# Graph network on one core: tiles moved from the counted part of stage 1 to that of stage 2, with passes, node pieces and first indices placed anew

## What is computed

```python
# layer 0: two SAGE convolutions (mean over the in-edges), then residual and layernorm
h = relu(x @ Ws1 + mean_agg(x, src, dst) @ Wn1 + b1)
h = h @ Ws2 + mean_agg(h, src, dst) @ Wn2 + b2
x = layernorm(x + h)
# layer 1: an edge network, messages summed by dst, then residual and layernorm
ef  = (relu(edge_attr @ We1 + be1) @ We2 + be2) * sigmoid(edge_weight @ Wt + bt)
msg = relu(concat([x[src], ef]) @ Wm1 + bm1) @ Wm2 + bm2
out = layernorm(segment_sum(msg, dst) + x + x)      # all in float32
```

## Time and profile before

| | |
|---|---|
| median of 3 runs | 7867.11 us (7864.79 to 7884.57) |
| profiled execution | 7882.65 us, span 7881.0 us |
| busy in the span | PE 76%, DVE 62%, ACT 48%, POOL 73% |
| first gathers of the stages | 3.58, 2279.25 and 3908.13 us |
| last gathers of stages 1 and 2 | 2206.78 and 3857.70 us |

### The profile page before, as it was taken

How to read it: one execution, slowest core, us unless ns; L and a number is a source line. 1 busy time by engine, 2 the same in 40 slices (tenths; PEclk the granted TensorE clock), 3 DMA queues, 4 the chain that set the end, 5 groups by cost and what they waited for, 6 DMA issues and landing times. The chain is left out here.

```text
span 7881.0 us, 109150 instructions
## 1 busy us (share of the span) xinstructions
PE 5987.7 (76%) x32520; PEld 3927.2 (50%) x32520; DVE 4860.4 (62%) x9745; ACT 3780.1 (48%) x6514; POOL 5733.1 (73%) x5857
## 2 busy tenths in 40 slices
PE   5778888888768788887677777777777777777777
PEld 4555555555545555565444444444444444444444
DVE  8999888888745555555365455555555555555555
ACT  2111121222120000000177777777888888888887
POOL 7777776666547777777577777777777777777776
PEclk8888998999879989898788888888888888888888
DMA  4466777887768898898644444444444444444443
GB/s 123 145 208 227 241 258 257 288 286 269 258 206 301 299 307 299 299 313 301 207 131 133 129 134 130 135 133 132 133 134 134 134 133 136 133 138 137 135 134 105
DMA packets 651285, 1524.09 MB, mean 193 GB/s; under 512 B 162961, under 2 KB 346917, under 8 KB 643014
## 3 DMA queue, kind: packets, MB, share of 16 engines
q1 hardware_dynamic: 463491, 1133.19, 42.7%
q0 software_dynamic: 187200, 383.76, 17.2%
HBM read 1374.92 MB, written 141.47 MB: 192 GB/s over the span
## 5 line engine op out<-in xcount | busy, mean ns | idle before, releaser
L1709 POOL DMA_INDIRECT messages_rows<-y_d,src_idx x3125 | 2991.6, 957 | 1001.5 <-issue 944.4
L1112 POOL DMA_INDIRECT sum_x_rows<-in_x,sum_x_edges x1525 | 1577.4, 1034 | 628.1 <-issue 434.4
L1112 POOL DMA_INDIRECT sum_z_rows<-z_d,sum_z_edges x1200 | 1162.7, 969 | 488.2 <-issue 345.4
L1787 PE MATMUL messages_p_msg<-Wm_e,messages_gated 128*128 128x128 f32 x6250 | 1009.9, 328 | 511.0 <-DVE messages_below L1926 510.5
L1787 PEld LDWEIGHTS messages_p_msg<-Wm_e,messages_gated 128*128 128x128 f32 x6250 | 934.3, 237 | 889.3 <-issue 888.0
L1916 DVE TENSOR_TENSOR messages_p_msg<-messages_p_msg,messages_rows 128x1024 f32<-128x1024 f32 x391 | 481.3, 1231 | 1172.0 <-DMA messages_rows<-y_d,src_idx 930.3
L1216 PE MATMUL sum_x_build<-sum_x_key_hot,sum_x_low_hot 128*128 128x490 bf16 (+2 forms) x2900 | 831.2, 373 | 300.3 <-DVE sum_x_counts L1412 289.9
L1307 ACT CAST sum_x_hot<-sum_x_hot 128x320 bf16<-128x320 f32 x305 | 139.7, 458 | 1739.8 <-DVE sum_x_hot L976 1739.8
L1812 ACT ACTIVATE messages_hot<-iota,rel 128x128 bf16<-128x128 f32 x3125 | 950.2, 389 | 0.0
L1236 PE MATMUL sum_z_p_loaded<-sum_z_split,sum_z_counts 128*128 128x384 bf16 x2744 | 799.3, 350 | 161.5 <-DMA sum_z_split<-z_parts_d 156.2
L1799 PE MATMUL messages_p_edge<-messages_hid,We 128*128 128x512 f32 x1564 | 804.2, 640 | 0.0
(11 more groups left out here) (274 smaller groups left out, 9251.5 us busy)
## 6 DMA issues: line engine op xcount, KB each, us to landing
sum_x_split<-x_parts_d SPq DMA_DIRECT2D x392, 675.5 KB
sum_z_split<-z_parts_d SPq DMA_DIRECT2D x392, 675.5 KB
messages_when<-in_edge_weight SPq DMA_DIRECT2D x391, 512.0 KB, 4.1
messages_attr<-in_span_attr SPq DMA_DIRECT2D x391, 256.0 KB
counts_d<-sum_x_counts SPq DMA_DIRECT2D x392, 224.0 KB
sum_z_counts<-counts_d SPq DMA_DIRECT2D x56, 1568.0 KB
messages_rows<-y_d,src_idx POOLq DMA_INDIRECT x3125
sum_x_rows<-in_x,sum_x_edges POOLq DMA_INDIRECT x1525
```

The source lines that it names most:

```text
L1112: nc.gpsimd.indirect_dma_start(out=rows[:, s % depth, j, :], out_offset=None, in_=table, in_offset=bass.IndirectOffsetOnAxis(ap=edges[:, b ...
L1709: nc.gpsimd.indirect_dma_start(out=rows[:, g % SPAN_DEPTH, j, :], out_offset=None, in_=d["y"], in_offset=bass.IndirectOffsetOnAxis(ap=src_ ...
L1787: last = nc.tensor.matmul(p_msg[:, j * P:(j + 1) * P], gated[:, g % SPAN_GATEDS, j * P:(j + 1) * P], t.Wm_e[:], start=True, stop=True)
```

## The change

Five edits, all in the tables and in which tile a gather reads its indices from.

1. Stage 1 counts tiles 0 to 1500 (25 blocks, 13 pieces from counted blocks, units up to slot 308) and gathers 1625. Stage 2 loads 25 blocks and counts 1500 to 1925 itself, in 17 blocks; it still gathers 1200.
2. In stage 2, 18 intervals between ends of its own blocks hold the 25 passes, so 7 of them are cut in two halves with a pass in each, spread evenly; before, all 14 intervals were cut in two, for 28 passes.
3. In stage 1 pieces that start after slot 278 (`units_by - LATE`) follow each other by 4 slots for 5, and pieces of gathered nodes may start 2 slots after their last group for 4.
4. The indices of the first 25 gathers of stage 2 are loaded in stage 1 (`second_src`), and those of the first 24 gathers of stage 3 in stage 2 (`third_src`).
5. The load of `xT` of a stage 1 piece goes from step 0 to step 1.

```diff
-SPAN_LOADS, SPAN_AHEAD = 4, 3
+SPACING_LATE, LATE = 4, 30
+SPAN_LOADS, SPAN_AHEAD, SPAN_FIRST = 4, 3, 3
...
+        extra = plan.loaded - len(ends)
...
-            until = from_ + 16 if last else ends[j + 1]
-            halves = [(from_, until)] if len(left) <= blocks - j + 1 else [(from_, (from_ + until) // 2), ((from_ + until) // 2, until)]
+            double = ((j + 1) * extra + len(ends) // 2) // len(ends) > (j * extra + len(ends) // 2) // len(ends)
+            until = from_ + (16 if double else 8) if last else ends[j + 1]
+            halves = [(from_, (from_ + until) // 2), ((from_ + until) // 2, until)] if double else [(from_, until)]
...
+    def gathered_by(k):
+        tile = tiles * sqrt(min((PIECE * (k + 1) + 80) / m.N, 1.1))
+        return min(int((tile - end) / TILES) + 2, plan.groups)
...
-            tile = tiles * sqrt(min((PIECE * (k + 1) + 80) / m.N, 1.1))
-            ready.append(min(int((tile - end) / TILES) + 4, plan.groups + 2))
+            ready.append(gathered_by(k))
...
-        slot += spacing
+        slot += spacing if slot < units_by - LATE else SPACING_LATE
...
-        if s == 0:
+        if s == 1:
             load(sp, n, k)
...
-                if q == 0:
+                if q == 0 and (first or body):
                     pool.wait_ge(edges_in[body % EDGES_RING], 16 * (body // EDGES_RING + 1))
...
+                if s == UNROLL and first:
+                    sp.dma_start(t.second_src[:], d["edges"][:, second_from // BODY, 0]).then_inc(next_in, 16)
+                if s == UNROLL and not first:
+                    sp.dma_start(t.third_src[:], d["src_tiles"][:, 0:SPAN_FIRST * SPAN]).then_inc(next_in, 16)
...
-    first = make_plan(m, 0, 1600, 28, 14, 290, SPACING)
-    second = make_plan(m, 1600, 1925, 13, 20, 212, SPACING_SECOND, first)
+    first = make_plan(m, 0, 1500, 25, 13, 308, SPACING)
+    second = make_plan(m, 1500, 1925, 17, 20, 212, SPACING_SECOND, first)
```

More of the change, by code:

```diff
@@ L150, in make_plan @@
             from_ = plan.block_end[b]
-            plan.passes.append(([b], from_, min(26, plan.block_end[b + 1] - from_ - 2) if b + 1 < plan.blocks else 9))
+            plan.passes.append(([b], from_, min(26, plan.block_end[b + 1] - from_ - 2) if b + 1 < plan.blocks else 6))
     for together, from_, length in plan.passes:
@@ L161, in nodes_until @@
         return m.N * (tile / tiles) ** 2
+    def gathered_by(k):
+        tile = tiles * sqrt(min((PIECE * (k + 1) + 80) / m.N, 1.1))
+        return min(int((tile - end) / TILES) + 2, plan.groups)
     ready, plan.first_block, plan.last_block = [], [], []
     for k in range(m.PIECES):
-        if k < flat:
-            from_ = next((b for b in range(plan.blocks) if nodes_until(plan.block_at[b]) + P >= PIECE * k - 10), plan.blocks - 1)
+        from_ = next((b for b in range(plan.blocks) if nodes_until(plan.block_at[b]) + P >= PIECE * k - 10), plan.blocks)
+        last = next((b for b in range(plan.blocks) if nodes_until(plan.block_at[b + 1]) >= PIECE * (k + 1) + 10), plan.blocks - 1)
+        if k < flat and from_ < plan.blocks:
             plan.first_block.append(from_)
-            last = next((b for b in range(plan.blocks) if nodes_until(plan.block_at[b + 1]) >= PIECE * (k + 1) + 10), plan.blocks - 1)
             plan.last_block.append(last)
@@ L179, in make_plan @@
         plan.start[k] = slot
-        slot += spacing
-    plan.slots = plan.start[plan.order[-1]] + PIECE_STEPS
+        slot += spacing if slot < units_by - LATE else SPACING_LATE
+    plan.slots = max(plan.start[plan.order[-1]] + PIECE_STEPS, plan.groups + 2)
     assert [k for k in plan.order if k >= flat] == list(range(flat, m.PIECES))
@@ L287, in vector_checks @@
         then(nc.vector.tensor_tensor(above[:, 0:plan.blocks], block_f[:], above[:, 0:plan.blocks], ALU.is_lt))
-        then(nc.vector.tensor_scalar(above[:, plan.blocks:], block_f[:], float(plan.flat * PIECE - P), None, ALU.is_gt))
+        then(nc.vector.tensor_scalar(above[:, plan.blocks:], block_f[:], float(plan.touched * PIECE - P), None, ALU.is_gt))
         then(nc.vector.tensor_reduce(found[:, 4:5], above[:], axis=AX.X, op=ALU.max))
-        then(nc.vector.memset(above[:, 0:plan.blocks], float(plan.flat * PIECE)))
-        for k in reversed(range(plan.flat)):
+        then(nc.vector.memset(above[:, 0:plan.blocks], float(plan.touched * PIECE - P)))
+        for k in reversed(range(plan.touched)):
             if plan.first_block[k]:
@@ L978, in one_hot, with sum_neighbours @@
         rel.unsqueeze(2).to_broadcast([P, TILES, WIN]), ALU.is_equal)
-def sum_neighbours(nc, m, plan, d, t, table, parts, first, nodes_step, sb, pb, sem):
+def sum_neighbours(nc, m, plan, d, t, table, parts, first, nodes_step, second_from, sb, pb, sem):
     C = PARTS if first else 1
@@ L1106, in _ @@
                 wait_for(pool, sums_ready, s - depth + 1)
-                if q == 0:
+                if q == 0 and (first or body):
                     pool.wait_ge(edges_in[body % EDGES_RING], 16 * (body // EDGES_RING + 1))
                 pool.sem_inc(gathers_started, 1)
+                sources = edges[:, body % EDGES_RING, 0] if first or body else t.second_src[:]
                 for j in range(TILES):
@@ L1181, in _ @@
             placed.sync_last(sp)
+            sp.wait_ge(next_in, 16)
             if first:
@@ L1708, in _ @@
                     at = g * SPAN + j
+                    sources = t.third_src[:] if g < SPAN_FIRST else src_idx
                     nc.gpsimd.indirect_dma_start(
                         out=rows[:, g % SPAN_DEPTH, j, :], out_offset=None, in_=d["y"],
-                        in_offset=bass.IndirectOffsetOnAxis(ap=src_idx[:, at:at + 1], axis=0)).then_inc(rows_arrived[g % SPAN_DEPTH], 16)
+                        in_offset=bass.IndirectOffsetOnAxis(ap=sources[:, at:at + 1], axis=0)).then_inc(rows_arrived[g % SPAN_DEPTH], 16)
             for q in range(SPAN_DEPTH):
@@ L2163, in gnn @@
         t.zeros = sb("zeros", [P, 1], FP32)
+        t.second_src, t.third_src = sb("second_src", [P, BODY], I32), sb("third_src", [P, SPAN_FIRST * SPAN], I32)
         t.columns, t.iota = sb("columns", [P, 1024], FP16), sb("iota", [P, P], FP32)
-        run("sum_x_", sum_neighbours, nc, m, first, d, t, d["x"], d["x_parts"], True, first_nodes)
+        run("sum_x_", sum_neighbours, nc, m, first, d, t, d["x"], d["x_parts"], True, first_nodes, second.end)
         where_needed("any_x_", sum_neighbours_generally, nc, m, d, t, d["x"], True, first_nodes)
-        run("sum_z_", sum_neighbours, nc, m, second, d, t, d["z"], d["z_parts"], False, second_nodes)
+        run("sum_z_", sum_neighbours, nc, m, second, d, t, d["z"], d["z_parts"], False, second_nodes, None)
         where_needed("any_z_", sum_neighbours_generally, nc, m, d, t, d["z"], False, second_nodes)
```

11 lines of the change are left out of this document (8 added, 3 removed).

## The result

The changed kernel takes 7837.61 us (median of 20 runs, 7828.46 to 7857.74), the kernel before 7867.86 us (20 runs, 7843.35 to 7884.66): ratio 0.9963, 95% interval 0.9957 to 0.997. That is 30 us faster, with 61 forecast. Its profiled execution took 7828.46 us with a span of 7826.8 us, so the two profiled executions differ by 54 us and the medians by 30.

The account below looks back on a forecast made before the run. It took stage 1's second half as bound by the DVE and PE chain, stage 3 by POOL's gathers; -47 - 19 - 4 + 22 - 6 - 7 = -61 us gave 7806 us from the median 7867.1, range 7735 to 7865.

Parts of the forecast that it names:

- What bounds stage 1: Second half of stage 1: bound by the DVE and PE chain, not POOL; per slot they fall to 5.6 and 5.75 us.
- stage 1 stays chained: Rival for stage 1: DVE and PE wait per unit, not by load; 125 us of waits left, 7901 us; chance 0.08.
- Stage 1, term -47: Stage 1 up to its last gather: 1625 gathers at 1.309 us plus 30 us of waits, 2157 us for 2204.
- Tail of stage 1, -19: After stage 1's last one-hot: three late pieces left for five save 19 us; closer spacing does nothing.
- Start of stage 2, -4: Start of stage 2: POOL already has its indices and need not wait for their load, saving 4 us.
- Stage 2, gathers, +22: Gathers of stage 2: 8 us more for 100 added key one-hots, 14 us of new waits in 7 cut intervals.
- The one-hot's price: POOL's gathers: each key one-hot adds 0.08 us, so moving 100 takes 8 us from stage 1, adds 8 to stage 2.
- Tail of stage 2, -6: End of stage 2: one piece fewer starts after the last group, saving about 6 us.
- Start of stage 3, -7: Start of stage 3: with indices loaded ahead, POOL's gathers start with the other engines, saving 7 us.
- The same saving gives 7806: Whole kernel: the 61 us saving, summed against the profiled 7882.65 us, is taken from the median 7867.1 us, giving 7806.
- The short passes stall POOL: Rival for stage 2: lead used up in each cut interval, 7 x 8 us more waited, 7862 us; chance 0.12.
- Both stages relax: Rival: stage 1's waits go wholly, lighter DMA takes 50 us of stage 2's, 7726 us; chance 0.10.

Follow-up runs that it names:

- second pair of traces: Kernel before and changed kernel each run and profiled once more, unchanged: medians 7866.27 us and 7835.62 us, traces 7868.03 us and 7838.56 us.
- the doubled one-hots: Changed kernel with VectorE making every key one-hot of stage 2 a second time, into a buffer that nothing reads: 7864.24 us, ratio 0.9998.

## Why the prediction was off in size

The direction was right and the time lay inside the range, but only half of the forecast saving came. By the prediction's own steps, with the second pair of traces, which stands for the medians:

- **What bounds stage 1: right.** The second half was held by DVE and PE, and both fell by slot as worked out (5.64 and 5.56 us for 5.6 and 5.75). The rival "stage 1 stays chained" is out: the delay went to zero in both traces of after. The first gather of stage 2 came at 2217.84 us for the 2205 expected, as the next terms explain.
- **Stage 1, term -47: -38 measured** (-41 in the first pair, -33 by all traces), through two errors that nearly cancel, which is luck. I left 30 us of waits, and none stayed. But the gather's pace was read wrong. I took busy time plus "issue", 1.319 us, and called the rest, 192 us, waits. A pause that ends in a wait holds the usual 0.3 us too, and the row books all of it as wait. The delay was 163 us and the pace (2203 - 163) / 1525 = 1.338; after has 2162 / 1625 = 1.330. The step down, 0.008, is close to the forecast 0.010 (whether fewer one-hots make it is another matter, see below); the base was 0.02 too low, 31 us over the stage.
- **Tail of stage 1, -19: -16.** Fewer late pieces fit it; the closer spacing, which I had put at nothing, shows no gain beyond the spread of 44 to 54 us.
- **Start of stage 2, -4: 0.** The indices were there, and POOL still started 3.4 us after ScalarE (4.3 before), and 8.4 to 8.7 us after the last work. The row names no releaser but issue, and the kernel before with the loads ahead showed the same. What it waits for I can't say.
- **Stage 2, gathers, +22: +34** (+18 in the first pair, +32 by all traces). In proportion this is the term that was mis-sized most. It held +8 for one-hots and +14 for waits. Waiting grew by 30 us (delay 43 to 73) and the pace by about 4. The step that failed is "With 7 such intervals I take 2 us of new wait in each". The working ahead of it was about right (41 us of PE forecast in a first pass, 43 found; an interval 15 to 20 us behind, where that at slot 141 took 102 us, from 3151 to 3253, for 12 slots of 6.5), but I took the lead of 8 groups to hide nearly all of it. In the first three intervals of the first trace it hid all but 1 us, and in each of the last four 10 to 22 us were lost. Why it held in those and not in these, the runs don't show; already before the change the waits lay in the second half. A slot more in each short pass took 44 us away, 6 for each cut interval, more than the 30 they had added; cuts at the front, where they follow each other with no whole pass between to catch up, added 57. Lighter DMA paid in PE's waits for chunks (156.2 to 73.6 us), but the build bank, which I had named as the other strain and given no term, took 48.7 back, and PE has 36 us more to do.
- **The one-hot's price.** The line through the earlier trace rows gave 0.08 us each; the doubled one-hots 0.03 to 0.04, so the moved hundred cost 4 us and not 8. The stages differ in more than one-hots (stage 1 gathers from another table), and a line through two stages put that on them. The Trainium skill (SBUF — State Buffer, "Who interferes with whom") gives the shared ports to whichever of GpSimd and a two-port VectorE operation issues first, and blocks the other for the whole instruction. No row names the one-hot's mode. It lasts 0.38 to 0.43 us here, and the run shows about a tenth of that in POOL's time, so the measurement decides against a whole one-hot as the price for gathers. (The moved tiles kept their 588 columns and 0.38 us, so by that rule, too, stage 2 would have paid 38 us and not 43, and the forecast would not have moved.)
- **Tail of stage 2, -6: -7. Start of stage 3, -7: -6.** Right.
- **"The same saving gives 7806".** The sum was made against an execution 15 us above its median. Its waits were longer than those of the second trace in both stages (delay 163 and 51, then 152 and 43), and a change that removes waits saves less from a typical run. Of the 31 us between -61 and -30, by the second pair, the gathers of stage 2 hold 12, stage 1's gathers 9, its tail 3, the start of stage 2 4, and the rest is a stage 3 that was 3 us longer. By all traces stage 1's gathers missed by 14 and stage 2's by 10, so they share the blame.
- **The rivals.** "The short passes stall POOL" was the right mechanism at 6 us an interval instead of its 8 more, so the truth lay between forecast and that rival. (The 6 us are an average: single intervals cost 0 to 22.) "Both stages relax" is half true: stage 1's waits went wholly, and of stage 2's most go (delay 15 to 32 left) once the short passes are a slot longer.

The best version that ran is the changed kernel with the short passes a slot longer, 7794 us, 44 us ahead of the change and 74 of the kernel before; the one with all passes longer and 9 buffers, 7793 us, can't be told from it.

## What to carry to other kernels

Where work that is fixed in total is spread over slots, price each burst by the time its stretch takes at least, and not by the mean: a pass that reads a whole table has a floor of its own however few products it does, and short passes with a fixed pause between them give away that pause too, as far as the longer passes show it. Look whether the load that a change moves meets a single buffer at its new place, as the build bank here. A bounding engine's waits, as a profile books them, hold its usual pause as well, so take pace and delay from the starts and not from "busy plus issue". And profile a kernel twice before working out terms of 10 us: one execution here was 15 us off its median, in just the waits that the change was to remove.

## What was not expected of the hardware

- The usual pause of POOL between two gathers, 0.30 us, stands inside a wait that the rows book: the 9 waits of after in 1000:2000 make 2.7 us, 0.3 each and so no delay, and before's 192 us of waits in stage 1 were 163 us of delay.
- A key one-hot of 0.38 to 0.43 us on VectorE costs the gathers beside it 0.04 us at the most (983 ns for 969 with 425 more of them).
- With its indices already there, POOL begins a stage 8.4 to 9.5 us after the last work of the stage before, at stage 2, and 5.3 us after it at stage 3. The traces don't show why they differ.
- A pass over the table with 98 products took 36 to 44 us in 4 or 5 slots, with the DMA engines 85 to 94% busy at 287 to 324 GB/s, beside 18 to 30 gathers.
